# Where the second experts' down biases are accumulated: from the down products' banks to the projection's banks

## The chip, the cores and the metric

The kernel runs on one core of a Trainium2 chip. The metric is the device time of one execution in microseconds (us). Before the change the median of three runs is 2679.3 us (2676.52 to 2686.96).

## The reference, cut to what matters

Two layers, each a layer norm followed by attention plus a mixture of experts on the same normalised input. The change concerns the second layer: a linear attention, whose output goes through a projection, and eight experts whose down products have a bias that is weighted by the gates.

```python
xn = _layernorm(x, axis=-1)
x = x + _L1_attn_ref(xn, ...) + _L1_ffn_ref(xn, ...)

def _L1_attn_ref(x, qkv_w, qkv_b, proj_w, proj_b):
    ...
    out = out.transpose(0, 2, 1, 3).reshape(b, n, c)
    return out @ proj_w.T + proj_b

def _L1_ffn_ref(...):
    ...
    act = (up + 1.0) * gate * jax.nn.sigmoid(SWIGLU_ALPHA * gate)
    out = jnp.einsum('nei,edi->ned', act, down_proj) + down_proj_bias
    y = jnp.einsum('ned,ne->nd', out, combine.astype(out.dtype))
```

The input has 8 batches of 1024 tokens with 128 channels. The bias part of `y` is `combine @ down_proj_bias`, (1024 x 8) times (8 x 128) for each batch. Since both terms are added to the same `x`, it may be added to either.

## The kernel before, in words

The five engines run programs written out by hand, joined by semaphores. Each batch goes through the first attention (softmax, 64 tiles of scores), the first experts (two of eight, gathered in blocks), the second norm and router, and then the second experts with the linear attention beside them; then the next batch starts. Every engine works its list in order; nothing is reordered by a planner.

The second experts' stage is cut into 32 units: 8 experts, two slices of 128 hidden channels each, two halves of 512 tokens each. The stages of a unit are:

- TensorE, `gate_up(u)` (L1399): six matmuls of 512 columns into two of the banks 0 to 3.
- ScalarE (L771, L784) and VectorE (`limits`, L1191, and `product`, L1204): limits, silu, product.
- GpSimd (L620): the product times the gate's row, into one of five buffers; from unit 5 on it waits for the down product of four units before.
- TensorE, `down(u)` (L1406): one float32 matmul of 512 columns, accumulated over all units in bank 4 (first half of the tokens) or 5 (second half). The result has channels on the partitions.

TensorE's list is the loop at L1436: in step u it issues `gate_up(u)`, then `down(u - 4)`, then one step of the linear attention (`flow_step(u)`, L1678). In step 4, ahead of the first down product, stands `down_biases` (L1409, matmul on L1414): for each half, weights `b_down` (8 x 128) and 512 columns of the transposed gates `gate_wT` (8 x 1024), with `start=True`; the down products then accumulate on them with `start=False`. The `flow_step` of step 4 waits for VectorE's L1234 and issues the ones-matmuls L1683.

In step 28 (`FLOW_PROJ`) `flow_step` issues the projection, L1731: for each of 8 token tiles one float32 matmul with the attention's transposed output (128 x 128) as weights and `w_proj` (128 columns) as the moving operand, into banks 6 and 7; here tokens are on the partitions. A semaphore tells of each half of four tiles. VectorE adds the halves to `x_mid` (L1295) and goes on with the limits of unit 29. In step 29 the next batch's key projection (L1355) follows, after both additions.

After step 35 ScalarE copies banks 4 and 5 (L668), TensorE turns them back to tokens on partitions (L1451), and VectorE adds them to `x_mid` too (L1034).

One float32 matmul of the program is two weight loads and two matmul instructions in the trace. So L1414 has 4 instructions a batch, L1731 has 16, and a down product 2.

Of the kernel before, what the change touches and what calls it, by code (L numbers as in the profile page):

```python
# [13 lines left out]
P = 128  # L14
# [3 lines left out]
D = 128  # L18
BANK = 512
HALVES = SEQ // BANK  # L20
# [74 lines left out]
DOWN_LAG = 4  # L95
# [71 lines left out]
def two_layer_kernel(nc, ins, out):  # L167
    with ExitStack() as ctx:
        def sb(name, shape, dt=F32):
            return ctx.enter_context(nc.sbuf_tensor(name, shape, dt))  # L170

        def signal(name, per=0, start=0):
            return Signal(ctx.enter_context(nc.semaphore(name)), per, start)
# [43 lines left out]
        heads_out, heads_outT = tmp, room[:, 6 * SEQ:7 * SEQ]  # L217
# [25 lines left out]
        gate_wT = probs[0:E, 1, :]  # L243
# [20 lines left out]
        ffn_h = [probs[:, slot, c * BANK:(c + 1) * BANK] for slot in (0, 2) for c in range(2)] + [ffn_h4]  # L264
# [35 lines left out]
        w_down = [sb(f"w_down{l}", [P, E * FH, D]) for l in range(2)]  # L300
# [7 lines left out]
        b_down = sb("b_down", [E, D])  # L308
        w_qkv = sb("w_qkv", [P, 3 * D])
        b_qkv = sb("b_qkv", [P, 3 * D])  # L310
        w_proj = sb("w_proj", [P, D])
# [22 lines left out]
        ps = ctx.enter_context(nc.psum_tensor("ps", [P, 8, BANK], F32))  # L334
# [85 lines left out]
        gateT_ready = signal("gateT_ready", 1)  # L420
# [894 lines left out]
        def _(pe):  # L1315
# [4 lines left out]
            for h in range(H0):  # L1320
                mm = nc.tensor.matmul(ps[0:DC + 1, 0, h * DC:(h + 1) * DC], uq_T[:, h, :], uk_T[:, h, :],
                                      start=True, stop=True)
# [5 lines left out]
            for h in range(H0):  # L1328

                nc.tensor.matmul(ps[:, 5, 0:D], b_uv[:, h:h + 1].to_broadcast([P, P]), wo_heads[:, h, :],  # L1330
                                 start=(h == 0), stop=(h == H0 - 1))
# [3 lines left out]
            for c in range(2):  # L1335
                last = nc.tensor.matmul(ps[:, 2 + c, :], dq_T,
                                        absorbed[0:DC, 4 * c:4 * c + 4, :].rearrange("p a b -> p (a b)"),
                                        start=True, stop=True)
# [37 lines left out]
            def gates_transpose(b):  # L1376
                pe.wait_ge(gate_ready.sem, gate_ready.at(b, 1))
                for n in range(NT):
                    mm = nc.tensor.transpose(ps[0:E, 4 + n // 4, (n % 4) * P:(n % 4 + 1) * P], gate_w[:, n, :],
                                             ident[:, :])  # L1380
                mm.then_inc(gateT_mm.sem, 1)

            def experts(b, beside, next_queries):
                def gate_up(u):
                    f, c = u // HALVES, u % HALVES
                    if u >= 2:

                        pe.wait_ge(gate_lim.sem, gate_lim.at(b, u - 1))
                        pe.wait_ge(up_lim.sem, up_lim.at(b, u - 1))
                    if u == 0:  # L1390
                        pe.wait_ge(o_added.sem, o_added.at(b, 3))
                        pe.wait_ge(x_low_ready.sem, x_low_ready.at(b, 1))
                    if c == 0:
                        slot = f % CHUNK_SLOTS
                        pe.wait_ge(w_loaded[slot].sem, w_loaded[slot].at(b, 16 * (f // CHUNK_SLOTS + 1)))
                    half = slice(c * BANK, (c + 1) * BANK)
                    for k, bank in enumerate((u % 2, 2 + u % 2)):
                        for part, (h, tokens) in enumerate(((0, x_high), (0, x_low), (1, x_high))):
                            mm = nc.tensor.matmul(ps[:, bank, :], w_split[:, f % CHUNK_SLOTS, h, k * P:(k + 1) * P],  # L1399
                                                  tokens[:, half], start=(part == 0), stop=(part == 2))  # L1400
                    mm.then_inc(gu_ready.sem, 1)

                def down(u):
                    f, c = u // HALVES, u % HALVES
                    pe.wait_ge(h_ready.sem, h_ready.at(b, u + 1))
                    nc.tensor.matmul(ps[:, 4 + c, :], w_down[1][:, f, :], ffn_h[u % 5], start=False,  # L1406
                                     stop=(f == E * FH - 1)).then_inc(down_done.sem, 1)

                def down_biases():  # L1409

                    pe.wait_ge(gateT_ready.sem, gateT_ready.at(b, 1))

                    for c in range(HALVES):
                        nc.tensor.matmul(ps[:, 4 + c, :], b_down[:, :], gate_wT[:, c * BANK:(c + 1) * BANK],  # L1414
                                         start=True, stop=False)

                def qkv_tile(n):
                    if n >= 2:
                        pe.wait_ge(z_ready.sem, z_ready.at(b, n - 1))
                    nc.tensor.matmul(ps[:, 6 + n % 2, 0:3 * D], xT[1][:, n * P:(n + 1) * P], w_qkv[:, :],  # L1420
                                     start=True, stop=True).then_inc(qkv_mm.sem, 1)

                pe.wait_ge(logits_taken.sem, logits_taken.at(b, 1))
                pe.wait_ge(latent_ready.sem, latent_ready.at(b, 1))
                qkv_tile(0)
                qkv_tile(1)
                gate_up(0)
                gate_up(1)
                gates_transpose(b)
                gate_up(2)  # L1430
                for n in range(2, 6):
                    qkv_tile(n)
                gate_up(3)
                for n in range(6, NT):
                    qkv_tile(n)
                for u in range(UNITS + DOWN_LAG):  # L1436
                    if EARLY_UNITS <= u < UNITS:
                        gate_up(u)
                    if u == DOWN_LAG:
                        down_biases()  # L1440
                    if u >= DOWN_LAG:
                        down(u - DOWN_LAG)
                    if u < UNITS:
                        beside(u)

                next_queries()
                pe.wait_ge(keys_ready.sem, keys_ready.at(b, 2))
                for n in range(NT):
                    if n % 4 == 0:
                        pe.wait_ge(yT_ready.sem, yT_ready.at(b, n // 4 + 1))  # L1450
                    mm = nc.tensor.transpose(ps[:, 6 + n // 4, (n % 4) * P:(n % 4 + 1) * P], y_T[:, n * P:(n + 1) * P],  # L1451
                                             ident[:, :])
                    if n % 4 == 3:
                        mm.then_inc(y_mm.sem, 1)
# [72 lines left out]
            for index in range(BATCH):  # L1527
                b = Sequence(index)
# [149 lines left out]
                def flow_step(u):  # L1678

                    if u == FLOW_SUMS:  # L1680
                        pe.wait_ge(qk_ready.sem, qk_ready.at(b, 1))
                        for n in range(NT):
                            mm = nc.tensor.matmul(ps[:, 6, 0:2 * D], ones, qkv[:, n, 0:2 * D], start=(n == 0),  # L1683
                                                  stop=(n == NT - 1))
                        mm.then_inc(sums_mm.sem, 1)
                    if u == FLOW_SUMS2:
                        pe.wait_ge(weighted_q.sem, weighted_q.at(b, 1))
                        pe.wait_ge(weighted_k.sem, weighted_k.at(b, 1))
                        for n in range(NT):
                            mm = nc.tensor.matmul(ps[:, 7, 0:2 * D], ones, weighted[:, n, :], start=(n == 0),  # L1690
                                                  stop=(n == NT - 1))
                        mm.then_inc(sums_mm.sem, 1)
                    if u in (FLOW_SUMS2, FLOW_SUMS2 + 1):
                        c = u - FLOW_SUMS2
# [3 lines left out]
                        for i in range(4):  # L1698
                            mm = nc.tensor.transpose(ps[:, 6, i * P:(i + 1) * P], weighted[:, 4 * c + i, 0:D],
                                                     ident[:, :])  # L1700
                        mm.then_inc(qnT_mm.sem, 1)
                    if u == FLOW_KV:
# [4 lines left out]
                        for n in range(NT):  # L1707
                            nc.tensor.matmul(ps[:, 6, 0:D], qkv[:, n, D:2 * D], v_comp[:, n, :], start=(n == 0),
                                             stop=(n == NT - 1))
                        nc.tensor.matmul(ps[:, 7, 0:NT * H1], ones, source_exp, start=True, stop=True  # L1710
                                         ).then_inc(kv_mm.sem, 1)
                    if u == FLOW_OUT:
                        pe.wait_ge(kv_ready.sem, kv_ready.at(b, 1))
                        pe.wait_ge(qnT_ready.sem, qnT_ready.at(b, 2))
                        for n in range(NT):
                            mm = nc.tensor.matmul(ps[:, 6 + n // 4, (n % 4) * D:(n % 4 + 1) * D],
                                                  q_normT[:, n * P:(n + 1) * P], kv, start=True, stop=True)
                            if n % 4 == 3:
                                mm.then_inc(heads_mm.sem, 1)
                    if u == FLOW_HEADS:  # L1720
                        for n in range(NT):
                            if n % 4 == 0:
                                pe.wait_ge(heads_ready.sem, heads_ready.at(b, n // 4 + 1))
                            mm = nc.tensor.transpose(ps[:, 6 + n // 4, (n % 4) * P:(n % 4 + 1) * P],
                                                     heads_out[:, n, :], ident[:, :])
                            if n % 4 == 3:
                                mm.then_inc(headsT_mm.sem, 1)
                    if u == FLOW_PROJ:
                        pe.wait_ge(headsT_ready.sem, headsT_ready.at(b, 2))
                        for n in range(NT):  # L1730
                            mm = nc.tensor.matmul(ps[:, 6 + n // 4, (n % 4) * D:(n % 4 + 1) * D],  # L1731
                                                  heads_outT[:, n * P:(n + 1) * P], w_proj[:, :], start=True, stop=True)
                            if n % 4 == 3:
                                mm.then_inc(proj_mm.sem, 1)

# [4 lines left out]
                def next_queries():  # L1740

                    if index + 1 < BATCH:
                        pe.wait_ge(gate_lim.sem, gate_lim.at(b, UNITS))
                        pe.wait_ge(up_lim.sem, up_lim.at(b, UNITS))
                        queries(0)

                experts(b, flow_step, next_queries)


# [71 lines left out]
```

## Time and profile before

| | |
|---|---|
| median of three runs | 2679.3 us |
| profiled execution, its own time | 2676.29 us |
| its span | 2674.3 us |
| mean granted TensorE clock | 0.967 |
| TensorE busy | 2462.1 us, 92% of the span |
| VectorE busy | 2073.9 us, 78% |
| ScalarE busy | 1632.9 us, 61% |
| GpSimd busy | 724.6 us, 27% |

PE is TensorE's matmul, PEld its weight load, DVE VectorE, ACT ScalarE, POOL GpSimd. L1414 is line 1414 of the kernel. A matmul's duration includes the time until its result is out, so durations of a stream overlap; the distance from start to start says how fast it goes. "Idle before" is the engine's idle time in front of an instruction, with what ended it; "issue" there means that nothing the profile shows was waited for. The granted clock is 1.00 at 2.4 GHz and 0.50 at 1.2 GHz.

### The profile page before, as it was taken

The numbers are of one execution on the slowest core, as the hardware profiler recorded it, in microseconds if no ns is written. First come the engines' busy times: TensorE is split into PE (matmuls) and PEld (weight loads), VectorE is DVE, ScalarE is ACT, GpSimd is POOL, SyncE is SP. The second block draws the span as 40 slices with busy tenths as digits, with TensorE's granted clock in tenths as the row PEclk, the third lists the DMA queues.
The fourth block names the chain that finished last, engine by engine and source line by source line (L and its number), as shares of the span: only waits on it lengthen the run. The fifth ranks groups of instructions, "written<-read, shape, count | busy, mean of one in ns | idle before, by whom it ended". The sixth has DMA issues, their size and how long they took to land.

```text
span 2674.3 us, 67343 instructions
## 1 busy us (share of the span) xinstructions
PE 2462.1 (92%) x26752; PEld 1795.2 (67%) x26752; DVE 2073.9 (78%) x3553; ACT 1632.9 (61%) x2872; POOL 724.6 (27%) x601
## 2 busy tenths in 40 slices
PE   4989999999999999999988999899998999999998
PEld 2767657776666766667656676676765767667765
DVE  4958878688777887778876778768788687885976
ACT  2757457565566656666566655667456575575845
POOL 1211342204322052220522215212152122520235
PEclk8999999999999999999999999999899999999999
DMA  6110211102111031110211112011121111211022
GB/s 237 41 33 10 88 55 41 40 3 103 40 40 40 3 107 37 40 40 29 87 30 44 36 42 79 29 44 32 45 75 32 45 29 61 68 31 46 21 72 63
DMA packets 93370, 136.25 MB, mean 51 GB/s; under 512 B 10111, under 2 KB 55240, under 8 KB 92552
## 3 DMA queue, kind: packets, MB, share of 16 engines
q1 hardware_dynamic: 84872, 115.16, 13.3%
q0 software_dynamic: 8192, 16.79, 2.1%
q8 instruction: 219, 3.59, 0.6%
q14 instruction: 87, 0.71, 0.1%
HBM read 101.31 MB, written 30.61 MB: 49 GB/s over the span
## 4 chain that ended last, share of the span: by engine, by line
PE 57%; DVE 21%; issue 14%; ACT 6%; POOL 2%; DVEq 0%; ACTq 0%; POOLq 0%
PE ps L1399 9%; PE ps L1537 7%; DVE neg_max L1061 7%; PE ps L1477 6%; PE ps L1577 5%; DVE probsT L1076 5%; PE ps L1406 4%; ACT probs L722 4%; PE ps L1562 4%; PE ps L1628 4%; PE ps L1499 3%; PE ps L1420 2%; DVE ffn L1204 2%; PE ps L1372 2%; PE ps L1488 1%
## 5 line engine op out<-in xcount | busy, mean ns | idle before, releaser
L722 ACT ACTIVATE probs<-ps,neg_max 128x1024 f32<-128x1024 f32 x512 | 571.2, 1116 | 156.8 <-DVE neg_max L1061 155.1
L1061 DVE TENSOR_REDUCE neg_max<-ps 128x1 f32<-128x1024 f32 x512 | 624.6, 1220 | 31.6 <-PE ps L1537 20.6
L1537 PE MATMUL ps<-keys,q_parts 64*128 64x512 f32 x3072 | 505.0, 433 | 39.2 <-ACT probs L722 37.0
L1399 PE MATMUL ps<-q_parts,w_split 128*128 128x512 f32 x1536 | 467.0, 440 | 17.3 <-ACT ffn L771 9.6
L1562 PEld LDWEIGHTS ps<-ident,probs 64*128 64x128 f32 x8192 | 339.7, 140 | 122.8 <-ACT probs L722 52.7
L620 POOL TENSOR_TENSOR probs<-ffn,q_parts 128x512 f32<-128x512 f32 x208 | 297.3, 1432 | 382.7 <-DMA q_parts<-gate_rows 149.7
L1399 PEld LDWEIGHTS ps<-q_parts,w_split 128*128 128x128 f32 x1536 | 286.8, 192 | 164.3 <-issue 62.8
L1562 PE MATMUL ps<-ident,probs 64*128 64x64 f32 x8192 | 345.8, 224 | 41.6 <-ACT probs L722 35.5
L1537 PEld LDWEIGHTS ps<-keys,q_parts 64*128 64x128 f32 x3072 | 256.9, 189 | 181.0 <-ACT probs L722 86.2
L1076 DVE COPY probsT<-ps 128x512 f32<-128x512 f32 x512 | 350.4, 684 | 20.6 <-PE ps L1562 18.9
L1577 PE MATMUL ps<-probsT,latent 128*32 128x128 f32 x8192 | 332.1, 282 | 27.5 <-DVE o_latent L1054 21.3
L771 ACT ACTIVATE ffn<-ps,room_of_gate 128x512 f32<-128x512 f32 x256 | 174.9, 683 | 252.9 <-PE ps L1399 252.8
L704 ACT COPY probsT<-ps 128x512 f32<-128x512 f32 x512 | 296.5, 579 | 37.7 <-PE ps L1562 36.9
L578 POOL TENSOR_TENSOR rstd<-var_eps,minus_half 128x8 f32<-128x8 f32 (+2 forms) x25 | 33.0, 1319 | 907.1 <-DVE var_eps L865 907.1
L1577 PEld LDWEIGHTS ps<-probsT,latent 128*32 128x32 f32 x8192 | 198.9, 110 | 71.9 <-issue 44.2
L1406 PE MATMUL ps<-probs,w_down 128*128 128x512 f32 x416 | 213.3, 597 | 10.1 <-POOL probs L620 9.3
L1477 PE MATMUL ps<-w_res,q_parts 128*128 x552 | 183.0, 441 | 20.5 <-DVE q_parts L1136 11.9
L1154 DVE TENSOR_TENSOR ffn<-ffn,ps 128x256 f32<-128x256 f32 x184 | 77.3, 420 | 148.6 <-ACT ffn L746 139.6
L784 ACT ACTIVATE ffn<-ffn,silu_bias 128x512 f32<-128x512 f32 x256 | 185.0, 723 | 7.7
L1204 DVE SCALAR_TENSOR_TENSOR ffn<-ffn 128x512 f32<-128x512 f32 x176 | 166.1, 947 | 22.0 <-issue 22.0
L1191 DVE TENSOR_SCALAR ffn<-ps,b_up 128x512 f32<-128x512 f32 x176 | 131.4, 747 | 44.0 <-PE ps L1399 41.8
L746 ACT ACTIVATE ffn<-ps 128x256 f32<-128x256 f32 x184 | 71.4, 388 | 121.7 <-PE ps L1477 121.7
(217 smaller groups left out, 3334.0 us busy)
## 6 DMA issues: line engine op xcount, KB each, us to landing
w_split<-w_parts SPq DMA_DIRECT2D x132, 256.0 KB, 2.6
q_parts<-gate_rows SPq DMA_DIRECT2D x64, 512.0 KB, 3.9
y_rows<-probs SPq DMA_DIRECT2D x40, 256.0 KB, 2.2
x_in<-in_x SPq DMA_DIRECT2D x9, 512.0 KB, 4.3
w_parts<-q_parts SPq DMA_DIRECT2D x2, 2048.0 KB, 13.7
out<-x_mid SPq DMA_DIRECT2D x8, 512.0 KB, 3.2
ffn<-in_gate_up SPq DMA_DIRECT2D x1, 2048.0 KB, 8.9
probsT<-in_gate_up SPq DMA_DIRECT2D x1, 2048.0 KB, 13.1
```

The lines of the kernel that those rows point to most:

```text
L620: nc.gpsimd.tensor_tensor(ffn_h[u % 5], ffn_gu[:, u % 3, :], gate_bc[:, e % GATE_SLOTS, c * BANK:(c + 1) * BANK], ALU.mult).then_inc(h_rea ...
L704: nc.scalar.copy(half_of(t, 0), half_turned(t, 0)).then_inc(low_copied.sem, 1)
L722: nc.scalar.activation(probs[:, t % 3, :], banks(2 * (t % 2)), ACT.Exp, bias=neg_max[:, t % 4:t % 4 + 1], accum_out=row_sum[:, g % 2, t % ...
L1061: nc.vector.tensor_reduce(neg_max[:, t % 4:t % 4 + 1], banks(2 * (t % 2)), X, ALU.max, negate=True).then_inc(max_ready.sem, 1)
L1076: nc.vector.tensor_copy(half_of(t, 1), half_turned(t, 1)).then_inc(high_copied.sem, 1)
L1204: nc.vector.scalar_tensor_tensor(ffn_gu[:, u % 3, :], ffn_u[u % 3], 1.0 - LIMIT, ffn_s[:, u % 3, :], ALU.max, ALU.mult).then_inc(gu_done.s ...
L1399: mm = nc.tensor.matmul(ps[:, bank, :], w_split[:, f % CHUNK_SLOTS, h, k * P:(k + 1) * P], tokens[:, half], start=(part == 0), stop=(part ...
L1406: nc.tensor.matmul(ps[:, 4 + c, :], w_down[1][:, f, :], ffn_h[u % 5], start=False, stop=(f == E * FH - 1)).then_inc(down_done.sem, 1)
L1477: mm = nc.tensor.matmul(ps[:, j % 2, :], xs_parts[x][:, at], w_res_flat[:, bass.ds(first[j] * 4 + h * 2 * F, 2 * F)], start=(part == 0), s ...
L1537: mm = nc.tensor.matmul(ps[:, 2 * (t % 2) + c, :], q_parts[rows, j, q, n * P:(n + 1) * P], keys[rows, k, :], start=(part == 0), stop=(part ...
L1562: mm = nc.tensor.transpose(ps[:, turn_bank(t, c), k * HQ:(k + 1) * HQ], probs[rows, t % 3, k * P:(k + 1) * P], ident[rows, rows])
L1577: nc.tensor.matmul(ps[DC * j:DC * (j + 1), 7, 0:P], latent[:, k, :], probsT[:, (g % 2) * QUAD + j, k * P:(k + 1) * P], start=(k == 0), sto ...
```

## The change

The two bias matmuls of 512 columns ahead of the first down product are gone. The first down product of each bank starts the accumulation, and the one of unit 0 waits for the gates' copy. In the projection each token tile gets a second float32 matmul behind the first, accumulated onto it: weights are that tile's transposed gates (8 x 128), the moving operand is `b_down` (8 rows, 128 columns).

```diff
                 def down(u):
                     f, c = u // HALVES, u % HALVES
                     pe.wait_ge(h_ready.sem, h_ready.at(b, u + 1))
-                    nc.tensor.matmul(ps[:, 4 + c, :], w_down[1][:, f, :], ffn_h[u % 5], start=False,
+                    if u == 0:
+                        pe.wait_ge(gateT_ready.sem, gateT_ready.at(b, 1))
+                    nc.tensor.matmul(ps[:, 4 + c, :], w_down[1][:, f, :], ffn_h[u % 5], start=(f == 0),
                                      stop=(f == E * FH - 1)).then_inc(down_done.sem, 1)
-
-                def down_biases():
-
-                    pe.wait_ge(gateT_ready.sem, gateT_ready.at(b, 1))
-
-                    for c in range(HALVES):
-                        nc.tensor.matmul(ps[:, 4 + c, :], b_down[:, :], gate_wT[:, c * BANK:(c + 1) * BANK],
-                                         start=True, stop=False)
...
-                    if u == DOWN_LAG:
-                        down_biases()
                     if u >= DOWN_LAG:
                         down(u - DOWN_LAG)
...
                         for n in range(NT):
-                            mm = nc.tensor.matmul(ps[:, 6 + n // 4, (n % 4) * D:(n % 4 + 1) * D],
-                                                  heads_outT[:, n * P:(n + 1) * P], w_proj[:, :], start=True, stop=True)
+                            at = ps[:, 6 + n // 4, (n % 4) * D:(n % 4 + 1) * D]
+                            nc.tensor.matmul(at, heads_outT[:, n * P:(n + 1) * P], w_proj[:, :], start=True, stop=False)
+                            mm = nc.tensor.matmul(at, gate_wT[:, n * P:(n + 1) * P], b_down[:, :], start=False, stop=True)
```

## Rows read from the trace of the kernel before

**Rows 1.** The page: span, TensorE's busy time, granted clock in 40 slices (tenths).
```profile
span 2674.3 us, 67343 instructions
...
PE 2462.1 (92%) x26752; PEld 1795.2 (67%) x26752; DVE 2073.9 (78%) x3553; ACT 1632.9 (61%) x2872; POOL 724.6 (27%) x601
...
PEclk8999999999999999999999999999899999999999
```

**Rows 2.** Chain of work that ended last, first batch, 270 to 395: start, us, what.
```profile
292.81 1.23 DVE probsT L1234
...
364.93 1.78 PE ps L1731 x16
...
369.64 1.27 POOL probs L620
```

**Rows 3.** Timeline, all engines, first batch, 282 to 300: start, us, engine, line.
```profile
289.15 1.29 POOL L620 TENSOR_TENSOR probs<-ffn,q_parts 128x512 f32<-128x512 f32 x1 [19.41 <-DMA q_parts<-gate_rows]
...
290.28 1.98 PE L1414 MATMUL ps<-probs,b_down 8*128 8x512 f32 x4
...
292.19 1.13 PE L1406 MATMUL ps<-probs,w_down 128*128 128x512 f32 x2
...
294.08 3.72 PE L1683 MATMUL ps<-probsT,ones 128*128 128x256 f32 x16 [0.77 <-DVE probsT L1234]
```

**Rows 4.** Who waited for whom on PE: us in total, times, longest.
```profile
PE ps L1683 <- DVE probsT L1234: 4.9, 8, 0.8
```

**Rows 5.** Timeline, weight loads of the first batch, 282 to 370.
```profile
290.28 0.29 PEld L1414 LDWEIGHTS ps<-probs,b_down 8*128 8x128 f32 x2 [0.37 <-issue]
...
290.81 0.19 PEld L1414 LDWEIGHTS ps<-probs,b_down 8*128 8x128 f32 x1 [0.24 <-issue]
...
291.24 0.18 PEld L1414 LDWEIGHTS ps<-probs,b_down 8*128 8x128 f32 x1 [0.24 <-issue]
...
292.19 0.30 PEld L1406 LDWEIGHTS ps<-probs,w_down 128*128 128x128 f32 x2 [0.76 <-issue]
...
363.68 0.42 PEld L1406 LDWEIGHTS ps<-ffn,w_down 128*128 128x128 f32 x2
```

**Rows 6.** Timeline of PE at the first attention's output, first batch, 256 to 262.
```profile
257.41 2.05 PE L1610 MATMUL ps<-w_o,o_latent 128*128 128x128 f32 x16
259.39 0.65 PE L1577 MATMUL ps<-probsT,latent 128*32 128x128 f32 x16
```

**Rows 7.** Timeline, all engines, first batch, 360 to 392, around and behind the projection.
```profile
363.91 1.02 PE L1406 MATMUL ps<-ffn,w_down 128*128 128x512 f32 x2
...
365.93 1.51 DVE L1295 TENSOR_TENSOR x_mid<-x_mid,ps 128x512 f32<-128x512 f32 x2 [0.47 <-PE ps L1731]
...
366.47 1.64 PE L1399 MATMUL ps<-q_parts,w_split 128*128 128x512 f32 x6
...
368.15 0.75 DVE L1191 TENSOR_SCALAR out_room<-ps,b_up 128x512 f32<-128x512 f32 x1 [0.71 <-PE ps L1399]
...
368.81 1.88 PE L1355 MATMUL ps<-xT_first,w_k 128*128 128x512 f32 x4
...
372.11 0.75 DVE L1191 TENSOR_SCALAR ffn<-ps,b_up 128x512 f32<-128x512 f32 x1 [2.61 <-PE ps L1399]
...
378.06 2.35 PE L1406 MATMUL ps<-probs,w_down 128*128 128x512 f32 x4 [1.16 <-POOL probs L620]
```

**Rows 8.** Stretches, batches 3 and 6: length, busy by engine (instructions), granted clock, DMA share, GB/s.
```profile
940.95:944.36 3.41, 3.38 (x8) 0.96 (x6) 3.41 (x4) 3.38 (x4) 2.15 (x3) 1.00 0.97 375
944.36:947.77 3.41, 2.97 (x7) 2.43 (x8) 2.06 (x3) 0.08 (x1) 2.77 (x2) 0.50 0.03 11
...
1927.40:1930.81 3.41, 2.61 (x6) 2.15 (x7) 2.41 (x3) 0.12 (x1) 2.78 (x2) 0.50 0.13 47
```

**Rows 9.** Timeline of PE: the ones-matmuls of batches 3 and 6.
```profile
944.80 5.17 PE L1683 MATMUL ps<-probsT,ones 128*128 128x256 f32 x16 [0.48 <-DVE probsT L1234]
...
1928.20 6.68 PE L1683 MATMUL ps<-probsT,ones 128*128 128x256 f32 x16 [0.81 <-DVE probsT L1234]
```

## The prediction

> **What bounds the kernel now.** I read the page first: TensorE is busy for 92% of the span, no other engine for more than 78% [rows 1]. So added TensorE time is suspect, but only where TensorE is what the next step waits for. The eight batches repeat one pattern, so I then read the chain of waits over the second experts' stage of the first batch [rows 2]. At the place from which the bias matmuls are taken, the chain runs over VectorE: L1234 (start 292.81, 1.23 us) releases the ones-matmuls L1683. At the place to which they go, it runs over TensorE: L1731 takes 1.78 us for 16 instructions, and the next units' L1399 and VectorE's and GpSimd's units follow it.
>
> TensorE's timeline around the old place [rows 3]: the four bias instructions (two float32 matmuls of 512 columns, each issued as two) start at 290.28, the first down product at 292.19, and L1683 at 294.08, with idle time before it. The view of all waits has this eight times, once per batch, 4.9 us in all [rows 4]. L1234 waits for no matmul of these: VectorE's and ScalarE's own units lie before it.
>
> **What one change of shape costs.** The weight-load rows [rows 5] show something that the busy times hide. Between 128-row matmuls the next weights are loaded under the running stream: L1406's first load starts at 363.68, before its matmul at 363.91 [rows 7]. Around L1414, whose weights have 8 rows, this stops. The loads start together with the matmuls (290.28 and 292.19) after a gap. From L1414's first instruction (290.28) to its third load (290.81, with the second matmul) are 0.53 us, where the steady step is 0.43 (290.81 to 291.24). From there to L1406 at 292.19 are 1.38 us, where three steps would end 0.09 earlier. So a switch costs 0.09 us of waiting and 0.10 us of open weight load, 0.19 to 0.20 together. The same holds for 128-column streams: L1610's 16 instructions, with a change of tile shape on either side, last from 257.41 to 259.39, 1.98 us [rows 6], where L1731's 16 of the same shape take 1.78: again 0.20, for the open load at its entry and the wait at its exit.
>
> **The change, part by part.**
>
> 1. Bias matmuls out of unit 4. TensorE loses 4 x 0.43 + 2 x 0.20 = 2.1 us a batch. None of it shortens the path: the ones-matmuls wait for L1234 in all eight batches, and the down product's earlier end serves nobody, since GpSimd looks at the down products only from unit 5 on. The cover is VectorE's chain up to 294.08. The moved wait for the gates' copy is long met; the first down product can start once GpSimd's first product ends (289.15 + 1.29 = 290.44 [rows 3]), so TensorE then idles from about 291.3 to 294.08, 2.8 us. Term: 0 (bounds: 0 and a gain of 2.1 if the chain view were wrong).
>
> 2. Streams into the projection. Eight more float32 matmuls of 128 columns are 16 instructions at 1.78/16 = 0.111 us: 1.78 us a batch.
>
> 3. Switches in the projection. The new matmuls alternate, tile by tile, with the 128-row ones, so each brings a switch in and a switch out: 16 x 0.196 = 3.1 us a batch (lower bound 0, if loads were hidden). The projection thus grows from 1.8 to 6.7 us.
>
> 4. Who waits. GpSimd and SP issue nothing more and no queue is moved past. VectorE waits for the projection in L1295, and behind it stand the limits and product of the next units. These need the next gate and up matmuls (L1399), which start after the projection too: VectorE idled for them until 368.15 and 372.11, ScalarE likewise [rows 7]. The key projection (368.81) waits for L1295's second half, which ends at 365.93 + 1.51 = 367.44, 1.4 us before; both shift alike. No idle time stands before TensorE's L1399 and L1355 behind the projection. The idle time before the last down products (1.16 us at 378.06 [rows 7]) is not slack: those wait for GpSimd's products, which the late L1399 delay as well. So terms 2 and 3 count in full: 4.9 us a batch, 39.2 us.
>
> 5. The clock. The granted clock is not constant. In the third batch it was 1.00 in 940.95 to 944.36 and 0.50 (1.2 GHz) in the next 3.4 us, though the matmul unit had been busy for 3.38 of the 3.41 us before [rows 8]; in that stretch lay the 8-row matmuls (from 941.29) and the wait for L1234. The sixth batch has it too, from 1927.40. L1683 then took 5.17 and 6.68 us instead of 3.72 [rows 3, 9]: a fall costs 1.45 to 2.96. I read this as busy time not being enough: 8 of 128 rows and open weight loads keep the array nearly empty. The new projection is 6.7 us of just that: of 0.83 us per tile only 0.21 are full-row streams. I expect the clock to fall in it in every batch, or nearly. The fall came 3.1 us after the first 8-row matmul (941.29 to 944.36); then some 3.5 us of the projection are left, which cost 3.5 more if all of it scales and I take 2.3, since waits need not scale; then dense work at 0.50 until the clock returns, 1.45. Estimate 3.7 us a batch, 29.6 (bounds 1.45, a fall at the end, and 3.5 + 2.96 = 6.5).
>
> 6. The clock at the old place. The 8-row work gives way to idle time, now unbroken for 2.8 us. Instead of two falls in eight batches I take four: 2 x 1.45 = 2.9 us (bounds 0 and 6 x 1.45 = 8.7).
>
> Sum: 39.2 + 29.6 + 2.9 = 71.7 us on the profiled execution's 2676.3, so 2748.0 us. The median shown, 2679.3, lies 0.1% above that execution, within the spread of the three runs.
>
> The Trainium skill (TensorE: Matmul & The Clock Gate, the clock gate and its failure modes) ties the low clock to idle gaps between bursts. By it alone the projection, which has no such gap, would keep its clock and the time be 2718; the third batch speaks against it.
>
> **Rivals.**
>
> *The clock holds.* If only idle time lowers it, the two falls seen are due to the gap before L1683, and term 5 goes: 2676.3 + 39.2 + 2.9 = 2718.4. For it: that gap stood in both stretches. Against: rows 8's 3.38 us busy, and the same gap in six other batches without a fall.
>
> *Switches hidden.* If an 8-row load could go under a 128-row stream, only the streams are paid: 8 x 1.78 = 14.2, so 2690.5. Against it: rows 5 and 6, at both stream lengths. The same page of the Trainium skill (what happens when a matmul is issued) says that weight loads are pulled ahead of running matmuls when row groups don't conflict or the background buffer is the target; by that this rival would be the rule, while the trace shows it for equal shapes alone.
>
> *Absorbed, so not slower.* If the end of the batch were set by GpSimd's chain (369.64 on, [rows 2]), TensorE's lateness would vanish in the idle time before the last down products as long as it stays under that idle time, and the 2.1 us at unit 4 might return: 2676 down to 2659. It decides at L1191 of unit 29: only if VectorE did not wait there for L1399. It did, 0.71 and 2.61 us [rows 7].
>
> **How the numbers follow.** Forecast, switches and clock: 0.66, 2748. Clock holds: 0.20, 2718. Switches hidden: 0.08, 2690, which is at the edge of what can be told from no change (about 0.5%, 13.4 us), half to each side. Absorbed: 0.06, of it 0.04 unchanged and 0.02 faster. So faster 0.02, same 0.08, slower 0.90. The forecast's own range is 2727 (term 5 at 1.45) to 2768 (most batches near the upper bound); with the second case it begins at 2712.
>
> **What would show it.** In the changed profile: L1414's rows are gone, and L1683 still starts about 1.3 us after L1234 with more idle before it. The projection lasts 6.5 us at full clock, each narrow pair about 0.4 us behind its neighbour, weight loads with idle time before them. VectorE's L1295 halves lie some 3 us apart. The clock row shows 0.50 in or right behind the projection in each batch, and the distance from projection to the batch's end grows by 1.5 to 4 us over that. I am wrong if the loads of the narrow matmuls start under the wide streams, if the clock stays at 1.00 there, or if the first GpSimd product after the projection is not later by as much as the projection is longer.

## The result and the profile after

The changed kernel takes 2741.59 us (median of four runs, 2736.64 to 2747.02), 1.0225 times the kernel before (95% interval 1.0192 to 1.0258); the four runs of the kernel before that were taken with it have the median 2683.13 us. Five further executions, with other runs of the kernel before beside them (median 2680.19 us), gave 2750.02 us and 1.0277 (1.0252 to 1.0303). It is slower in both, by 58.5 and 69.8 us between the medians. The forecast was 2748 us in 2712 to 2768.

The profiled execution took 2746.31 us. The page of the changed kernel, beside [rows 1]:

```profile
span 2744.5 us, 67543 instructions
...
PE 2516.7 (92%) x26848; PEld 1831.5 (67%) x26848; DVE 2072.8 (76%) x3553; ACT 1632.1 (59%) x2872; POOL 724.3 (26%) x601
...
PEclk7999999999999999999999999999999999999999
```

TensorE has 96 matmul instructions more (16 a batch added, 4 taken away) and is busy for 54.6 us more; the busy times of VectorE, ScalarE and GpSimd differ by 1.1 us at most, and the span is 70.2 us longer. TensorE's share stays at 92% in both, so the page alone does not say where the time went.

The old place, first batch, in the timeline of all engines (start, us, engine, line, and the idle time before). It answers to [rows 3]; the ones-matmuls are now L1675 and the down product L1408:

```profile
295.91 1.30 POOL L620 TENSOR_TENSOR probs<-ffn,q_parts 128x512 f32<-128x512 f32 x1 [19.12 <-DMA q_parts<-gate_rows]
...
297.26 1.12 PE L1408 MATMUL ps<-probs,w_down 128*128 128x512 f32 x2
...
299.57 1.21 DVE L1234 TENSOR_SCALAR probsT<-probsT 128x2048 f32<-128x2048 f32 x1
...
300.84 1.35 PE L1675 MATMUL ps<-probsT,ones 128*128 128x256 f32 x5 [2.46 <-DVE probsT L1234]
```

L1675 starts 1.27 us after L1234's start, exactly the distance of before (292.81 to 294.08). What the bias matmuls occupied has become idle time: 2.46 us in place of 0.77 (the prediction had put it at 2.8). The view of all waits gives it for the eight batches, beside [rows 4]:

```profile
PE ps L1675 <- DVE probsT L1234: 19.7, 8, 2.5
```

The new place, second batch, in TensorE's timeline. The projection's 128-row matmuls (L1724, called wide here) and the 8-row bias matmuls (L1725) alternate, two instructions each:

```profile
704.91 0.38 PE L1724 MATMUL ps<-w_proj,probsT 128*128 128x128 f32 x2
705.22 0.48 PE L1725 MATMUL ps<-b_down,probs 8*128 8x128 f32 x2
705.64 0.49 PE L1724 MATMUL ps<-w_proj,probsT 128*128 128x128 f32 x2
706.05 0.48 PE L1725 MATMUL ps<-b_down,probs 8*128 8x128 f32 x2
...
709.62 0.79 PE L1725 MATMUL ps<-b_down,probs 8*128 8x128 f32 x2
710.34 0.80 PE L1724 MATMUL ps<-w_proj,probsT 128*128 128x128 f32 x2
711.06 0.79 PE L1725 MATMUL ps<-b_down,probs 8*128 8x128 f32 x2
...
713.23 2.93 PE L1399 MATMUL ps<-q_parts,w_split 128*128 128x512 f32 x6
```

At full clock a pair of instructions starts 0.41 to 0.42 us after the one before it, where its streams alone would take 0.22. From 709 on the distance is 0.72, and the stretches of the same batch say why (length, busy by engine, granted clock before the two last columns):

```profile
705.68:709.07 3.39, 3.39 (x18) 2.42 (x17) 0.69 (x1) 0.01 (x1) 1.27 (x1) 1.00 0.00 0
709.07:712.48 3.41, 3.41 (x10) 2.32 (x10) 0.00 (x0) 0.00 (x0) 0.00 (x0) 0.50 0.00 0
712.48:715.90 3.42, 3.42 (x9) 2.65 (x9) 0.69 (x1) 0.00 (x0) 0.00 (x0) 0.50 0.00 0
715.90:719.31 3.41, 3.41 (x5) 1.34 (x4) 1.35 (x2) 1.41 (x2) 1.26 (x1) 0.50 0.25 77
719.31:722.70 3.39, 3.39 (x13) 2.09 (x12) 0.90 (x2) 2.21 (x4) 0.00 (x0) 1.00 0.00 0
```

TensorE is busy without a gap ahead of the fall (3.39 of 3.39 us, as the profile counts it; open weight loads between the streams count as busy), and the clock goes to 0.50 all the same. It stays there for 10 us, past the end of the projection.

The clock falls in every batch, at 3.2 to 6.4 us behind the projection's start. The table has distances between starts in the timelines, in us: from the projection to the next L1399, and from there to the transposes of the experts' sum (L1451, after the change L1443). The second profile is that of the last run below.

| batch | before | changed, first profile | changed, second profile |
|---|---|---|---|
| 1 | 1.70 + 15.49 | 6.59 + 17.03 | 6.71 + 16.91 |
| 2 | 1.70 + 15.50 | 8.32 + 18.42 | 6.95 + 18.31 |
| 3 | 1.70 + 15.50 | 8.88 + 17.76 | 6.63 + 17.00 |
| 4 | 1.70 + 15.50 | 9.01 + 17.61 | 8.59 + 18.10 |
| 5 | 1.71 + 15.49 | 6.94 + 18.32 | 6.79 + 16.83 |
| 6 | 1.71 + 15.49 | 6.86 + 18.43 | 6.71 + 16.91 |
| 7 | 1.70 + 15.49 | 6.82 + 16.79 | 6.86 + 18.41 |
| 8 | 1.70 + 14.71 | 8.80 + 17.06 | 6.94 + 17.53 |
| sum | 136.8 | 203.6 | 196.2 |

So 66.8 us of the 70.2 lie here in the first profile, 59.4 us in the second. In batch 1 of the first profile the clock fell only 0.15 us before the end of the projection: 6.59 us, 4.89 more than before, is nearly the price of streams and switches alone (the half clock has some 0.04 us of it). Eight times that is 39.1 us; the remaining 27.7 us (20.3 in the second profile) are the clock's.

At the old place, from the ones-matmuls to the projection, the first profile is 2.7 us shorter than before, because the clock fell there in one batch instead of two.

Most of what is left of the 70.2 us lies ahead of both places. The stretch from the program's start to the first L1399 took 277.1 us before and 284.2 here. The granted clock of the first 100 us (third number from the right), before and after:

```profile
0.00:100.00 100.00, 58.44 (x646) 41.44 (x648) 61.87 (x166) 42.98 (x61) 9.80 (x20) 0.90 0.44 159
...
0.00:100.00 100.00, 60.41 (x542) 41.86 (x542) 56.01 (x153) 38.08 (x51) 8.99 (x18) 0.81 0.44 159
```

This is not the change's. The second profile of the changed kernel has 279.0 us and a clock of 0.88, and the 128-row matmuls at the old place, with the projection untouched, have 283.8 us and 0.83. In the nine profiles it is 277.1 us at a clock of 0.90, 279.0 to 279.1 at 0.88, 281.2 at 0.85, and 283.8 to 284.2 at 0.83 and 0.81. Why the clock differs there is open. It can make up to 7 us between two executions; whether the spread of 10 us and more between unprofiled ones comes from it is not shown.

### The profile page after: what moved, and what is told of

The parts are those of the page before. It is cut to its first block, busy times and chain, and to the rows that moved or that the text cites. A ratio compares the mean times of both kernels' runs of the same rounds, so it can differ in the third digit from the quotient of the medians.

```text
span 2744.5 us, 67543 instructions
## 1 busy us (share of the span) xinstructions
PE 2516.7 (92%) x26848; PEld 1831.5 (67%) x26848; DVE 2072.8 (76%) x3553; ACT 1632.1 (59%) x2872; POOL 724.3 (26%) x601
## 3 DMA queue, kind: packets, MB, share of 16 engines
q0 software_dynamic: 8192, 16.79, 2.0%
## 4 chain that ended last, share of the span: by engine, by line
PE 53%; DVE 21%; issue 17%; ACT 7%; POOL 2%; DVEq 0%; DMA 0%; ACTq 0%; POOLq 0%
PE ps L1399 9%; DVE neg_max L1061 7%; PE ps L1469 6%; DVE probsT L1076 5%; PE ps L1529 5%; ACT probs L722 4%; PE ps L1569 4%; PE ps L1408 4%; PE ps L1620 4%; PE ps L1491 3%; PE ps L1554 3%; PE ps L1414 2%; DVE ffn L1204 2%; PE ps L1372 2%; PE ps L1480 1%
## 5 line engine op out<-in xcount | busy, mean ns | idle before, releaser
L1399 PE MATMUL ps<-q_parts,w_split 128*128 128x512 f32 x1536 | 476.5, 447 | 17.3 <-ACT ffn L771 9.6
L1399 PEld LDWEIGHTS ps<-q_parts,w_split 128*128 128x128 f32 x1536 | 292.1, 196 | 167.6 <-issue 64.5
L1408 PE MATMUL ps<-probs,w_down 128*128 128x512 f32 x416 | 218.8, 611 | 10.3 <-POOL probs L620 9.4
```

## The experiments

### The bias in neither place

```diff
-                            nc.tensor.matmul(at, heads_outT[:, n * P:(n + 1) * P], w_proj[:, :], start=True, stop=False)
-                            mm = nc.tensor.matmul(at, gate_wT[:, n * P:(n + 1) * P], b_down[:, :], start=False, stop=True)
+                            mm = nc.tensor.matmul(at, heads_outT[:, n * P:(n + 1) * P], w_proj[:, :], start=True, stop=True)
```

> The bias matmuls are in neither place (the bias term is left out). My theory: at the old place they cost the path nothing, since the ones-matmuls wait for VectorE; the time is that of before within 0.3%, with the ones-matmuls 1.3 us behind the start of VectorE's sigmoid step in each batch, as before, and some 2.5 us idle ahead of them; at most 4 us less if the two clock falls there go. Rival (their 2.1 us were on the path): 17 us less, about 2664, with the ones-matmuls earlier against VectorE's step.

2678.34 us, 1.0001 times before (0.9987 to 1.0016); the rival's 17 us less lie far outside that. TensorE's waits:

```profile
PE ps L1675 <- DVE probsT L1234: 19.6, 8, 2.5
```

The idle time is that of the changed kernel, and nothing was gained. The 2.1 us a batch of matmul time at the old place were free. The clock still fell at the ones-matmuls in two of eight batches (distance to the projection 72.4 and 72.1 us instead of 70.7).

### The change with 128 rows in the added matmuls

The bias tile gets 128 rows, of which 120 are zero, and the weights are the whole 128 rows of the buffer that holds the gates. The lines that make and zero the tile are left out here.

```diff
...
-                            mm = nc.tensor.matmul(at, gate_wT[:, n * P:(n + 1) * P], b_down[:, :], start=False, stop=True)
+                            mm = nc.tensor.matmul(at, gate_rows_all[:, n * P:(n + 1) * P], b_down[:, :], start=False, stop=True)
```

> As the change, but the added matmuls have weights and moving operand of 128 rows (the 120 rows of the bias below the 8 are zero), so there is no change of tile shape. My theory: only the streams stay, 16 x 0.111 = 1.8 us a batch, 14 us in all, 0.5% over before; the projection takes 3.6 us, loads run under the streams, the granted clock is 1.00 in it and behind it in all batches. Rival (the clock falls because the projection is long or accumulates, whatever the rows): half clock there in most batches and 30 us more, 2.2% over before less the switches' 0.9%.

2697.5 us, 1.0064 times before (1.0041 to 1.0087), so 17 us where 14 were expected; the interval (11 to 23 us) holds both. The pairs in the projection of the first batch, and the granted clock there:

```profile
371.54 0.38 PE L1729 MATMUL ps<-w_proj,probsT 128*128 128x128 f32 x2
371.76 0.39 PE L1730 MATMUL ps<-b_down,probs 128*128 128x128 f32 x2
371.98 0.39 PE L1729 MATMUL ps<-w_proj,probsT 128*128 128x128 f32 x2
...
375.02 1.64 PE L1404 MATMUL ps<-q_parts,w_split 128*128 128x512 f32 x6
```

```profile
371.50:375.00 3.50, 3.50 (x33) 3.46 (x32) 1.41 (x3) 0.79 (x2) 1.27 (x1) 1.00 0.00 0
375.00:378.40 3.40, 3.40 (x14) 2.18 (x13) 2.04 (x3) 1.41 (x2) 0.21 (x1) 1.00 0.19 44
```

The same number of matmuls, streams of the same length, as many accumulations; only the rows differ. A pair now takes 0.22 us instead of 0.41, the projection 3.48 instead of 6.59, and the clock fell in or behind it in none of the eight batches. The added matmuls have sixteen times as many rows, 120 of 128 against zeros, and the kernel is 44 us faster for it (2741.59 against 2697.5; 53 us against the 2750.02 of the second series). The clock still fell at the ones-matmuls in two batches (72.4 and 73.8 us to the projection), where this kernel has no bias matmuls either.

### Half the switches

The order of every second tile is turned round: wide, narrow, narrow, wide.

```diff
-                            nc.tensor.matmul(at, heads_outT[:, n * P:(n + 1) * P], w_proj[:, :], start=True, stop=False)
-                            mm = nc.tensor.matmul(at, gate_wT[:, n * P:(n + 1) * P], b_down[:, :], start=False, stop=True)
+                            two = [(heads_outT, w_proj), (gate_wT, b_down)]
+                            for k, (w, x) in enumerate(two if n % 2 == 0 else two[::-1]):
+                                mm = nc.tensor.matmul(at, w[:, n * P:(n + 1) * P], x[:, :], start=(k == 0), stop=(k == 1))
```

> As the change, with the order of every second tile turned round (wide, narrow, narrow, wide), so 8 switches instead of 16. My theory: at full clock the projection takes 1.8 + 1.8 + 8 x 0.2 = 5.1 us, so 3.4 us a batch over before, 27 us; the quiet stretch is shorter, so the clock falls in most batches but not all and comes back sooner: 10 to 25 us on top, 1.4 to 2.0% over before. Rival (the clock's part is fixed for each batch): 27 + 29 = 56 us, 2.1%. Rival (all of the change's time is in the switches): half of 44 us plus 14, 1.4%, with no half clock to be seen.

2710.23 us, 1.0114 times before (1.0092 to 1.0136), 31 us. At full clock the projection takes 5.03 us in this run:

```profile
371.29 0.38 PE L1726 MATMUL ps<-w_proj,probsT 128*128 128x128 f32 x2
371.60 0.71 PE L1726 MATMUL ps<-b_down,probs 8*128 8x128 f32 x4
372.24 0.71 PE L1726 MATMUL ps<-w_proj,probsT 128*128 128x128 f32 x4
372.88 0.71 PE L1726 MATMUL ps<-b_down,probs 8*128 8x128 f32 x4
...
376.32 1.64 PE L1399 MATMUL ps<-q_parts,w_split 128*128 128x512 f32 x6
```

Four instructions and one switch take 0.64 us, so a switch is 0.64 - 4 x 0.111 = 0.20. The projection's lengths at 16, 8 and 0 switches are 6.59, 5.03 and 3.48 us: 0.195 us for each switch between the first two (0.19 without the late fall in the 6.59) and 0.194 between the last two. What I expected of the clock was wrong, and the 31 us are below the 37 to 52 I had given: it fell in or behind the projection in two batches of eight, not in most, at 3.2 us each (5.81 + 17.90 and 5.84 + 17.09 against 5.03 + 15.49 and, in the last batch, 5.03 + 14.71). With 8 x 3.33 = 26.6 us for streams and switches that makes 33 us. The rival that puts all of the time in the switches gave 1.4% with no half clock: its 36 us are nearer than mine, but the two falls speak against it. At the ones-matmuls the clock fell in four batches.

### 128 rows at the old place

The kernel before, with the 128-row bias tile (made and zeroed as above).

```diff
...
-                        nc.tensor.matmul(ps[:, 4 + c, :], b_down[:, :], gate_wT[:, c * BANK:(c + 1) * BANK],
+                        nc.tensor.matmul(ps[:, 4 + c, :], b_down[:, :], gate_rows_all[:, c * BANK:(c + 1) * BANK],
```

> The kernel before, its bias matmuls at the old place with 128 rows (zeros below the 8). My theory: 0.4 us a batch of switches go, off the path; the clock no longer falls at the ones-matmuls, where it did in 2 of 8 batches: the same time or up to 4 us (0.15%) less, and the stretch from the ones-matmuls to the projection is 70.7 us in all eight batches. Rival (the idle time ahead of the ones-matmuls makes the clock fall): falls stay in about 2 of 8.

2676.52 us over 12 executions, 0.9992 times before (0.9978 to 1.0006): no difference that this can tell. From the ones-matmuls to the projection it took 70.66 to 70.68 us in all eight batches, so there was no fall, against two in eight before. Eight batches are few: at a rate of one in four, none in eight comes up by chance about once in ten times. The idle time ahead of the ones-matmuls is still there. The next two runs ask the same question more sharply.

### The bias matmuls four times at the old place, with 8 rows and with 128

```diff
-                        nc.tensor.matmul(ps[:, 4 + c, :], b_down[:, :], gate_wT[:, c * BANK:(c + 1) * BANK],
-                                         start=True, stop=False)
+                        for k in range(4):
+                            nc.tensor.matmul(ps[:, 4 + c, :], b_down[:, :], gate_wT[:, c * BANK:(c + 1) * BANK],
+                                             start=(k == 0), stop=False)
```

This is the run with 8 rows. The one with 128 has `gate_rows_all` and the 128-row tile in it. In both the result holds the bias four times.

> The kernel before with each bias matmul issued four times at the old place, so the bias counts four times; 8 rows as before. The engine streams without a pause for 6.9 us there instead of 1.7, with still only two switches. My theory (rows that are not used do not count as activity): the clock falls in it in all eight batches; the streams add 5.2 us less the 1.0 us idle, 34 us in all, and the falls 1.5 to 4 us a batch, so 45 to 65 us over before. Rival (busy time alone counts): no more falls than before, 34 us over.

> As the run with the bias matmuls four times, but with 128 rows (zeros below the 8). Same streams, no switch. My theory: 3.8 us a batch, 30 us over before, and the clock at 1.00 from these matmuls to the projection in all batches. Rival (what makes the clock fall there is the place or the length): falls as in its twin.

With 8 rows the profiled execution took 2750.58 us, 73 us over the 2677.36 of before, where 45 to 65 were expected. A second execution took 5064.32 us at a granted clock of 1.0; there is no profile of it, I can't explain it, and it is left out, so the time with 8 rows rests on one execution. With 128 rows it is 2711.15 us (median of 2708.65, the profiled one, and 2713.65), 1.0126 times before (1.0095 to 1.0156), 34 us, where 30 were expected. TensorE's timeline and the stretches of the first batch with 8 rows:

```profile
292.35 11.81 PE L1415 MATMUL ps<-probs,b_down 8*128 8x512 f32 x16
304.10 2.08 PE L1406 MATMUL ps<-probs,w_down 128*128 128x512 f32 x2
305.96 4.33 PE L1684 MATMUL ps<-probsT,ones 128*128 128x256 f32 x14
```

```profile
291.20:294.62 3.42, 3.42 (x12) 1.70 (x11) 3.42 (x4) 2.97 (x3) 2.44 (x2) 1.00 1.01 366
294.62:298.00 3.38, 3.38 (x6) 1.29 (x5) 3.01 (x4) 0.85 (x2) 2.47 (x2) 0.50 0.33 125
298.00:301.40 3.40, 3.40 (x5) 1.32 (x4) 0.00 (x0) 0.00 (x0) 0.97 (x1) 0.50 0.00 0
```

And with 128 rows:

```profile
292.01 7.03 PE L1420 MATMUL ps<-probs,b_down 128*128 128x512 f32 x16
298.87 1.02 PE L1411 MATMUL ps<-probs,w_down 128*128 128x512 f32 x2
299.73 3.62 PE L1689 MATMUL ps<-probsT,ones 128*128 128x256 f32 x16
```

```profile
291.20:294.60 3.40, 3.40 (x12) 1.79 (x11) 3.40 (x4) 3.16 (x4) 2.33 (x2) 1.00 1.02 370
294.60:298.00 3.40, 3.40 (x9) 1.50 (x8) 2.91 (x4) 0.66 (x1) 2.60 (x2) 1.00 0.26 100
298.00:301.40 3.40, 3.40 (x13) 2.25 (x12) 0.00 (x0) 0.00 (x0) 0.86 (x1) 1.00 0.00 0
```

TensorE streams without a pause in both, sixteen matmul instructions of 512 columns one after the other. With 8 rows the clock fell within them in all eight batches (2.3 to 5.4 us behind their start, for 6.8 or 13.7 us each time), with 128 rows in none. From the start of the experts' stage to the projection the eight batches together are 43 us longer with 8 rows (201.7 + 573.0 against 167.1 + 564.6, in the distances from the first L1399 over the ones-matmuls to the projection), of which the two switches are 8 x 0.4 = 3. The other 40, 5.0 us a batch, are the clock's, above the 1.5 to 4 that I had expected; that is the miss. Here there are only two switches and no idle time in between, and the waits of the ones-matmuls for L1234 are gone from both profiles: 8 rows in place of 128 are enough to let the clock fall. How many rows would keep it, no run tells.

### The changed kernel once more

> The changed kernel once more, unchanged, for a second profile and a closer time. My theory: the granted clock is at half in or right behind the projection in all eight batches again, at other places within it; full-clock switches and streams cost 4.9 us a batch and the clock 3 to 4 us a batch, 60 to 68 us over before (2.2 to 2.5%). Rival (the falls in the first profile were partly chance): half clock at fewer than six projections, and some 2% or less.

2750.02 us, 1.0277 times before (1.0252 to 1.0303), some way over the 2.2 to 2.5% that I expected. The profiled execution, 2737.80 us, is the fastest of the five (up to 2763.85), so the clock's share read from it may be less than that of a typical one; the slower ones have a lower mean granted clock (down to 0.951 against 0.962), but no profile. The clock was at half in or behind the projection in all eight batches again; three of them in the second profile:

```profile
373.40:376.80 3.40, 3.40 (x9) 2.60 (x9) 0.74 (x2) 0.06 (x1) 0.00 (x0) 0.50 0.00 0
704.50:707.90 3.40, 3.40 (x10) 2.48 (x10) 0.69 (x1) 0.00 (x0) 0.00 (x0) 0.50 0.00 0
...
2711.50:2714.90 3.40, 3.40 (x10) 2.49 (x10) 0.69 (x1) 0.00 (x0) 0.00 (x0) 0.50 0.00 0
```

## Why the prediction was right, step by step

**Term 1, the bias matmuls taken away: 0.** Right. The kernel with the bias in neither place runs at 1.0001 times before. The idle time ahead of the ones-matmuls rose from 4.9 to 19.6 us over its eight batches, and the distance from them to the projection stayed at 70.7 us wherever the clock held.

**Terms 2 and 3, streams and switches: 39.2 us.** Right: 39.1. The projection was forecast at 6.7 us and takes 6.59 with the clock at full for all but its last 0.15 us. The streams alone are 3.48 - 1.70 = 1.78 us a batch (128 rows, no switch), and a switch is 0.19 to 0.195 us, with 8 switches and with 16. The two halves that make a switch up are a wait for the running stream (0.09 us in the prediction's rows) and a weight load that nothing covers (0.10). The Trainium skill (TensorEngine Tiling (Array Packing), Key Properties) says that changing the tiling mode drains the engine. The trace agrees: a step with a switch takes 0.41 to 0.42 us, one without 0.22, and the wait is about half of the difference.

**Term 4, all of it on the path.** Right. GpSimd's first product behind the projection's end:

```profile
369.63 1.27 POOL L620 TENSOR_TENSOR probs<-ffn,q_parts 128x512 f32<-128x512 f32 x1 [2.82 <-PE ps L1406]
...
382.57 1.26 POOL L620 TENSOR_TENSOR probs<-ffn,q_parts 128x512 f32<-128x512 f32 x1 [9.01 <-PE ps L1408]
```

It came 4.86 us after the projection's start before (364.77 to 369.63) and 11.04 us in the first batch of the changed kernel (371.53 to 382.57): 6.2 us later, more than the 4.9 that the projection grew by, since the L1399 behind it ran at half clock. No idle time took any of it up: TensorE's waits for GpSimd ahead of the down products are 9.4 us in all, 9.3 before. VectorE's two additions L1295 now start 3.3 us apart (374.93 and 378.23), as was forecast.

**Term 5, the clock at the projection: 29.6 us.** Right in kind and near in size: 27.7 us in the first profile, 20.3 in the second, that is 3.5 and 2.5 us a batch against 3.7; single batches lie between 1.5 and 4.7, within the stated 1.45 to 6.5. I had taken the rest of the projection as costing 2.3 us instead of 3.5 at half clock, two thirds more time. It is 0.72 us for a pair instead of 0.41, three quarters more. What brings the mean down is that in four batches of the first profile and seven of the second the clock fell near the projection's end, not in its middle. In the middle of it, at 3.2 to 4.2 us, the price was 4.5 to 4.7 us; where in the projection it falls, nothing in the rows of before could tell. By the rule of the Trainium skill (TensorE: Matmul & The Clock Gate, HAM oscillation) that ties the low clock to idle gaps, this term would have been nil; the 8-row matmuls repeated at the old place show that an engine that streams without a gap loses its clock as well, in eight batches of eight. The prediction named two reasons, the 8 rows and the open weight loads. That the rows alone suffice is shown there. What the open loads add is not: half the switches, with as many 8-row matmuls, brought the falls from eight to two, but the projection also became shorter by it, and no run has the switches without the 8 rows.

**Term 6, the clock at the old place: 2.9 us.** Wrong, though small. I put four falls in eight batches there, because the idle time becomes longer. In the first and second profile of the changed kernel there was one fall each, two with the bias in neither place, two with 128 rows in the projection and four with half the switches: 10 in 40 batches, against 2 in 8 before. That is the same rate, one in four: the 8-row matmuls had held the clock no better than idle time does, which was my own reading in term 5 and should have been applied here; then the term is 0. With two falls before (1.45 + 2.96) and one after (1.7) it was 2.7 us less in the profiled pair, not 2.9 more.

**The start.** Not in the prediction: 7.1 us of the profiled difference come from the part before the first batch's experts, where the clock depends on the execution. So the profiled execution of before was a fast one, and 2748, built on it, agrees with the medians of 2741.6 and 2750.0 partly by luck, because this offset the clock terms that came out smaller. Between the medians of the first series the change cost 58.5 us, not 71.7.

**The rivals.** That the switches' loads are hidden fell with 6.59 against 3.48 us. That the clock holds fell with eight falls in eight batches, twice. That the time is absorbed fell with term 4. The prediction gave the second of them 0.20 because the idle time ahead of L1683 stood in both stretches. That was misread: by [rows 8, 9] it began at 944.80 - 0.48 = 944.32 and 1928.20 - 0.81 = 1927.39, and the clock fell at 944.36 and 1927.40. So in neither batch did this idle time come before the fall, and the rows of before spoke more strongly against this rival than was said.

## What to carry to other kernels

Before a small matmul is moved into a series of large ones, compare the shapes: every change between an 8-row and a 128-row tile costs 0.2 us here, nearly as much as a whole float32 matmul of 128 columns (0.22), and padding the small one with zeros to 128 rows removes it. Take a matmul away from a place where the next step waits for another engine and you gain nothing; here the old place was free and the new one was on the path. And look at the granted clock beside the busy time: in this kernel a stretch in which TensorE is 100% busy, much of it on 8-row tiles, halved the clock of the dense work behind it.

## What the runs showed of the hardware that I had not expected

The clock can be lost with rows that are not used, at 100% busy time: sixteen matmul instructions of 512 columns with 8 rows brought it to half in eight batches of eight, the same with 128 rows, mostly zeros, in none. Zeros did not matter here; the number of rows did. And with half the switches the falls in or behind the projection dropped from eight to two in eight batches, far more than in proportion.
